# Rank rotation of gathered keys moved from the attention loop into a DRAM table built in the setup

## The reference, cut to what matters

```
_, idx = jax.lax.top_k(I, kk)                      # kk = 96, local ones are +inf
key_c = (c_kv @ W_uk)[bi, idx]
value = (c_kv @ W_uv)[bi, idx]
kr_sel = (x @ W_kr)[bi, idx]                       # 32 numbers per key
angles_k = jnp.arange(kk)[:, None] * theta[None, :] + delta     # rank, not position
key_r = _pope(kr_sel, angles_k[None, None, :, :])
```

## Time and profile before

| | |
|---|---|
| time, median of 3 runs | 1587.76 us (1586.1 to 1593.62) |
| span of the profiled execution | 1577.7 us |
| busy PE, DVE, ACT, POOL | 1150.9 (73%), 839.3 (53%), 752.6 (48%), 533.3 us (34%) |
| gathers on POOL | 496, 491.9 us busy |
| setup of this layer | about 498 to 617 us |
| first and last `row_max` | 665.5 and 1419.1 us |

### The profile page before, as it was taken

How to read it: one execution, slowest core, us unless ns; L and a number is a source line. 1 busy time by engine, 2 the same in 40 slices (tenths; PEclk the granted TensorE clock), 3 DMA queues, 4 the chain that set the end, 5 groups by cost and what they waited for, 6 DMA issues and landing times. The chain is left out here.

```text
span 1577.7 us, 20354 instructions
## 1 busy us (share of the span) xinstructions
PE 1150.9 (73%) x6768; PEld 804.0 (51%) x6768; DVE 839.3 (53%) x1759; ACT 752.6 (48%) x1801; POOL 533.3 (34%) x532
## 2 busy tenths in 40 slices
PE   6639958996999676367686776876777748287897
PEld 2138825672666222255564555655555536174554
DVE  2075555534553566466665665656556546034536
ACT  4722336771875544255444454445445434074425
POOL 2000000000000448366666666666666653600000
PEclk8559978995999566576656767667666555578999
DMA  5000000000003235112222122222222212200000
GB/s 181 0 1 0 0 0 0 1 0 0 1 1 87 76 90 139 46 32 56 54 54 56 32 56 54 57 55 47 41 57 55 54 25 41 57 5 27 1 1 27
DMA packets 74367, 61.82 MB, mean 39 GB/s; under 512 B 31570, under 2 KB 58900, under 8 KB 73764
## 3 DMA queue, kind: packets, MB, share of 16 engines
q1 hardware_dynamic: 58404, 36.28, 9.3%
q0 software_dynamic: 15872, 24.41, 6.7%
HBM read 52.51 MB, written 8.13 MB: 38 GB/s over the span
## 5 line engine op out<-in xcount | busy, mean ns | idle before, releaser
L542 POOL DMA_INDIRECT arena_lo<-key_table,idx_T x496 | 491.9, 992 | 304.0 <-issue 134.8
L576 PE MATMUL bank<-arena_lo 128*32 128x32 f32 (+6 forms) x1656 | 208.5, 276 | 116.1 <-ACT arena_hi L1280 66.6
L576 PEld LDWEIGHTS bank<-arena_lo 128*32 128x32 f32 (+5 forms) x1656 | 177.7, 166 | 168.4 <-issue 131.2
L555 POOL TENSOR_TENSOR arena_lo<-arena_lo 128x512 f32<-128x512 f32 x8 | 11.8, 1474 | 516.4 <-DVE arena_lo L1608 516.1
L856 PE MATMUL bank<-ident,arena_hi 128*96 128x128 f32 x512 | 113.4, 363 | 24.4 <-DVE arena_hi L1700 23.2
L1254 ACT ACTIVATE arena_hi<-bank 96x512 f32<-96x512 f32 x128 | 74.7, 583 | 113.6 <-remote 67.3
L1280 ACT ACTIVATE arena_hi<-bank 32x128 f32<-32x128 f32 x128 | 33.5, 262 | 194.0 <-remote 160.7
L1668 DVE SCALAR_TENSOR_TENSOR arena_lo<-arena_lo,iw 128x512 f32<-128x512 f32 (+4 forms) x114 | 76.1, 668 | 81.5 <-ACT arena_lo L1237 46.2
L1237 ACT ACTIVATE arena_lo<-bank 128x512 f32<-128x512 f32 (+4 forms) x152 | 76.5, 512 | 65.7 <-remote 30.9
L576 PE MATMUL bank<-index_k_hi,index_q 128*128 128x512 f32 (+5 forms) x160 | 94.0, 589 | 18.7 <-issue 17.0
L1710 DVE CUSTOM_DVE_ANT_0 arena_hi<-bank,score_mask 128x208 f32<-128x208 f32 x124 | 46.4, 374 | 106.9 <-issue 71.0
(11 more groups left out here) (257 smaller groups left out, 2484.3 us busy)
## 6 DMA issues: line engine op xcount, KB each, us to landing
arena_lo<-key_table,idx_T POOLq DMA_INDIRECT x496
arena_lo<-q_l SPq DMA_DIRECT2D x64, 64.0 KB
arena_lo<-q_lat SPq DMA_DIRECT2D x32, 128.0 KB
arena_lo<-q_g SPq DMA_DIRECT2D x64, 64.0 KB
h<-in_h SPq DMA_DIRECT2D x2, 1024.0 KB, 8.2
q_l<-arena_hi SPq DMA_DIRECT2D x8, 256.0 KB
q_g<-arena_hi SPq DMA_DIRECT2D x8, 256.0 KB
q_lat<-arena_hi SPq DMA_DIRECT2D x8, 256.0 KB
```

The lines of the kernel that those rows point to most:

```text
L542: pool.indirect_dma_start(out=G[b][:, q, :], out_offset=None, in_=key_table[0:index_width(i), :], in_offset=bass.IndirectOffsetOnAxis(ap=i ...
L576: return pe.matmul(out_, lhsT, rhs, start=start, stop=stop, **kw)
```

## The change

A table `rank_table` in DRAM (65536 rows of 64 numbers, 16.8 MB) holds, for each of the 2048 keys, 32 rows: the key turned by each rank from 64 to 95, and its latent beside it. Gathers read from it by index*32 + rank. What it adds in the setup for each chunk: on PE one product with a combining matrix, four small ones for latents, and eight products of 128 keys by 512 columns (`rank_turn`); eight copies of 128x512 from PSUM, four on ACT and four on DVE; eight latent copies on POOL; eight stores of 512 KB. The four transposes of raw keys are gone. POOL issues the gathers of tile 0 in chunk 1 and those of tile 1 in chunk 2, ahead of its part of chunk 3. What it changes in the loop: `rows_rotate` and a small DVE operation behind the row maximum are gone; two transposes of row pairs take the place of four; the scores of a group use two products with zero-padded query blocks (`QGz`) in place of four; one copy of turned probabilities replaces two; rows are of 64 numbers, not 96. Queries are double-buffered, attention lags its slot by 2 and not 7, and the picks end in slot 114. In front of the loop ACT waits for all stores and regroups the queries of tile 0. Semaphores of the linear attention are shared with an earlier layer.

```diff
+            def store_rank_rows(k, r):
+                b = 2 * (k % 2) + r
+                sp.wait_ge(t_halfs[r], k + 1)
+                sp.wait_ge(t_latb, 2 * k + r + 1)
+                sp.dma_start(rank_table[k * P * JG:(k + 1) * P * JG, :]
+                             .rearrange("(p r) w -> p r w", r=JG)[:, r * JG // 2:(r + 1) * JG // 2, :], tab[b])\
+                    .then_inc(t_store_t[b], 16)
...
+                sp.wait_ge(t_lats, c + 1)
+                sp.dma_start(lat_table[c * C:(c + 1) * C, :].rearrange("(b p) r -> p b r", p=P), lat_rows)\
+                    .then_inc(t_store_v, 16)
+                for j in range(4):
+                    for r in range(2):
+                        store_rank_rows(4 * c + j, r)
+                if c == 0:
+                    first_rows()
...
                     pool.indirect_dma_start(
-                        out=G[b][:, q, :], out_offset=None, in_=key_table[0:index_width(i), :],
+                        out=G[b][:, q, :], out_offset=None, in_=rank_table[0:JG * index_width(i), :],
...
+                pool.wait_ge(t_lats, c + 1)
+                for j in range(4):
+                    k = 4 * c + j
+                    for r in range(2):
+                        b = 2 * (k % 2) + r
+                        if k >= 2:
+                            pool.wait_ge(t_store_t[b], 16 * (k // 2))
+                        pool.tensor_copy(tab[b][:, :, DR:ROW], lat_rows[:, j:j + 1, :].to_broadcast([P, JG // 2, DC]))\
+                            .then_inc(t_latb, 1)
+                if c in (1, 2):
+                    table_stored(pool, c)
+                    gather(c - 1)
+            table_stored(pool, NT)
...
                     pe.wait_ge(t_iqs, 5 * c + 4)
-                    pe.wait_ge(t_rawd, c + 1)
+                    pe.wait_ge(t_kro, c + 1)
+                    mm(bank[7][0:ROW, :], key_comb, kro).then_inc(t_kl, 1)
+                    pe.wait_ge(t_iqs, 5 * c + 5)
+                    keys = raw[c % 2]
                     for j in range(4):
-                        last = pe.transpose(bank[7][:, j * ROW:(j + 1) * ROW], raw[c % 2][:, j * P:(j + 1) * P],
-                                            ident[0:ROW, 0:ROW])
-                    last.then_inc(t_rows, 1)
+                        last = mm(bank[2][:, j * DC:(j + 1) * DC], keys[:, j * P:(j + 1) * P], rank_turn[:, JG * DR:])
+                    last.then_inc(t_lat, 1)
+                    for j in range(4):
+                        for r in range(2):
+                            if j == 0:
+                                pe.wait_ge(t_qlats, 2 * c + r + 1)
+                            else:
+                                pe.wait_ge(t_halfs[r], 4 * c + j)
+                            mm(bank[3 + r], keys[:, j * P:(j + 1) * P], rank_turn[:, r * C:(r + 1) * C])\
+                                .then_inc(t_half[r], 1)
...
             def rows_turn(n):
-                pe.wait_ge(a_rot, n + 1)
+                i, g = n // NG, n % NG
+                if n < FIXED // GQ:
+                    pe.wait_ge(fixed_rows, 16 * QD)
+                else:
+                    gathers = i // 2 + (i % 2 == 1 or g >= FIXED // GQ)
+                    pe.wait_ge(gathered[i % 2][g], 16 * GQ // QD * gathers)
                 if n >= 2:
                     pe.wait_ge(a_gts, n - 1)
-                for j in range(4):
-                    last = pe.transpose(bank[2 + n % 2][0:ROW, j * P:(j + 1) * P], GR[n % 2][:, j, :], ident[:])
+                for p in range(2):
+                    pair = G[i % 2][:, 4 * g + 2 * p:4 * g + 2 * p + 2, :].rearrange("p j r -> p (j r)")
+                    last = pe.transpose(bank[2 + n % 2][:, p * P:(p + 1) * P], pair, ident[:])
                 last.then_inc(a_gt, 1)
...
             def scores(n):
                 i, g = n // NG, n % NG
                 pe.wait_ge(a_gts, n + 1)
-                pe.wait_ge(a_q, 4 * i + g // 2 + 1)
+                pe.wait_ge(a_q, 4 * i + 4)
                 if n >= 3:
                     pe.wait_ge(a_otc, n - 2)
                 s0 = max(i * P + g * GQ - LW, 0)
                 sb_, w = score_bank(n), NH * QD
-                mm(sb_[:, P:KEYS], QL[:, g, :], KL[:, s0:s0 + WIN])
-                for j in range(4):
-                    last = mm(sb_[j * w:(j + 1) * w, 0:P], QG[:, g, j * w:(j + 1) * w],
-                              GT[n % 2][:, j * P:(j + 1) * P], tile_position=(0, j * w))
+                mm(sb_[:, P:KEYS], QL[i % 2][:, g, :], KL[:, s0:s0 + WIN])
+                for p in range(2):
+                    last = mm(sb_[2 * w * p:2 * w * (p + 1), 0:P], QGz[i % 2][:, 2 * g + p, :],
+                              GT[n % 2][:, p * P:(p + 1) * P], tile_position=(0, 2 * w * p))
                 last.then_inc(a_s, 1)
...
-                fn(PTl[n % 2], score_bank(n)[0:WIN, P:2 * P], ACT.Copy)
-                fn(PTg[n % 2], score_bank(n)[:, 0:P], ACT.Copy).then_inc(a_pts, 1)
+                fn(PT[n % 2], score_bank(n)[:, 0:2 * P], ACT.Copy).then_inc(a_pts, 1)
...
+                act.wait_ge(t_halfs[1], NT)
                 for s in range(SLOTS):
                     n = s - ATTN_LAG
-                    if n == -4:
+                    if s == 0:
                         act.wait_ge(t_store_l, STORES_L * (NCH + 1))
                         act.wait_ge(t_store_q, STORES_Q * (NCH + 1))
                         act.wait_ge(t_store_g, STORES_Q * (NCH + 1))
-                        act.wait_ge(t_store_k, STORES_K * (NCH + 1))
+                        table_stored(act, NT)
+                        for part_ in range(4):
+                            queries_regroup(0, part_)
                     if 0 <= n + 1 < GROUPS:
...
-            def rows_rotate(n):
-                i, g = n // NG, n % NG
-                if n < FIXED // GQ:
-                    dve.wait_ge(fixed_rows, 16 * QD)
-                else:
-                    gathers = i // 2 + (i % 2 == 1 or g >= FIXED // GQ)
-                    dve.wait_ge(gathered[i % 2][g], 16 * GQ // QD * gathers)
-                if n >= 2:
-                    dve.wait_ge(a_gt, n - 1)
-                v.tensor_tensor(GR[n % 2], G[i % 2][:, 4 * g:4 * g + 4, :],
-                                rank_rope[:].unsqueeze(1).to_broadcast([P, 4, ROW]), ALU.mult).then_inc(a_rot, 1)
...
-        ATTN_LAG = NG - 1
-        PICK_SLOTS = NG * NT - 10
+        ATTN_LAG = 2
+        PICK_SLOTS = NG * (NT - 2) + ATTN_LAG
```

More of the change, by code:

```diff
@@ L52 @@
 NEG = -1e30
+FAR = 1e30
+HIGHEST = 3e38
 LOWEST = -3e38
@@ L89, in shape_tables @@
     for name, a in (("qg", q_g), ("ql", q_l)):
-        t["cos_" + name] = np.tile(np.cos(a), (NH, 1)).astype(f32)
-        t["sin_" + name] = np.tile(np.sin(a), (NH, 1)).astype(f32)
+        t["cos_" + name] = (-SCALE * np.tile(np.cos(a), (NH, 1))).astype(f32)
+        t["sin_" + name] = (-SCALE * np.tile(np.sin(a), (NH, 1))).astype(f32)
     c, s = np.cos(q_g), np.sin(q_g)
-    t["key_rope"] = np.concatenate([c, c, -s, s]).astype(f32)
-    a = (LW + np.arange(JG))[:, None] * theta[None, :]
-    row = np.concatenate([np.cos(a), np.cos(a), -np.sin(a), np.sin(a), np.ones((JG, DC))], axis=1)
-    t["rank_rope"] = np.tile(row, (P // JG, 1)).astype(f32)
+    t["key_rope"] = np.concatenate([c, c, -s, s, np.ones((DC, T))]).astype(f32)
+    eye, none = np.eye(half), np.zeros((half, half))
+    comb = np.zeros((RAW, ROW))
+    comb[0:2 * DR, 0:DR] = np.block([[eye, none], [none, eye], [eye, none], [none, eye]])
+    comb[2 * DR:RAW, DR:ROW] = np.eye(DC)
+    t["key_comb"] = comb.astype(f32)
+    turn = np.zeros((RAW, JG * DR + DC))
+    for r in range(JG):
+        c, s = np.diag(np.cos((LW + r) * theta)), np.diag(np.sin((LW + r) * theta))
+        turn[0:2 * DR, r * DR:(r + 1) * DR] = np.block([[c, none], [none, c], [-s, none], [none, s]])
+    turn[2 * DR:RAW, JG * DR:] = np.eye(DC)
+    t["rank_turn"] = turn.astype(f32)
     r = np.arange(P)
@@ L103, in shape_tables @@
     first = np.broadcast_to(x < LW, (P, WIN))
-    t["score_mask"] = np.where(np.concatenate([own, near], 1), 0, NEG).astype(f32)
-    t["score_mask_first"] = np.where(np.concatenate([own, first], 1), 0, NEG).astype(f32)
+    t["score_mask"] = np.where(np.concatenate([own, near], 1), 0, FAR).astype(f32)
+    t["score_mask_first"] = np.where(np.concatenate([own, first], 1), 0, FAR).astype(f32)
     p, s = np.arange(P)[:, None], np.arange(KTOP)[None, :]
@@ L256, in hybrid_kernel @@
         ROPE = at[0]
-        rope_tab = [part(4, C) for _ in range(NCH)]
-        cq, raw = [part(C, parts=DCQ) for _ in range(2)], [part(C, parts=ROW) for _ in range(2)]
+        rope_tab = part(4, C)
+        SCRATCH = at[0]
+        cq, raw = [part(C, parts=DCQ) for _ in range(2)], [part(C, parts=RAW) for _ in range(2)]
+        q_abs, mu = part(2, C), [part(2, C) for _ in range(2)]
+        assert at[0] == SCRATCH + 5120
+        tab = [part(JG // 2, ROW) for _ in range(4)]
+        G = [part(P // QD, ROW)]
+        lat_rows = part(4, DC)
         k_abs = part(C, parts=2 * DR)
```

(9 more changed lines are left out.)

329 lines of the change are left out of this document (191 added, 138 removed).

## The result

The changed kernel takes 1670.68 us (median of 4, 1657.23 to 1678.67) where the kernel before takes 1587.57: a ratio of 1.051, 95% interval 1.047 to 1.055. It is slower, as forecast, but by 83 us and not by 25. The profiled execution has a span of 1667.9 us beside 1577.7, 90.2 us more; it took 1669.73, so 1.8 us lie around a span. The 10.1 us that the prediction added were mostly the profiled execution of before being a quick one, so about 7 of the 90.2 us are not in the medians.

What follows compares the result with a forecast made beforehand. The prediction took gathers, the longest leg, plus POOL's pauses for PE's late signals to bound the loop. Span 1577.7 + 67 (setup) - 36 (loop) - 6 (its end) = 1602.7, with 10.1 1612.8 us; range 1562 to 1660.

Steps and rivals of the forecast that it cites:

- The 10.1 us that the prediction added: Whole kernel: time around the profiled span, 1587.76 us median against 1577.7 us span, added at the end.
- Forecast +67: Setup: first row maximum at 732 us against 665.49, so +67 us, bounds +45 and +89.
- 12.5 us more each: Setup: each chunk takes 12.5 us more, between 9.0 and 17.1 us of added PE work.
- PE's part of a slot gets about 20% shorter, DVE's as much: Loop slots: lighter PE and DVE work shortens POOL's pauses, taken as 0.32 us a slot.
- -36 for the loop: Loop: 112 slots beside gathers save 36 us through shorter and rarer POOL pauses; bounds 0 and -105.
- -6 for its end: After the last gather: some 14 slots lose 0.4 to 0.5 us each, -6 us.
- The upper bound of the gain, 105 us: Loop: 112 slots going from 6.04 to 5.1 us if POOL never pauses again, -105 us.
- Bursts at tiles 14 and 15: Loop: late indices again make the 32 gathers come in one 40 us burst, two bursts as before; 0 change.
- D: Rival: setup worse, signals held beside tile 1's gathers, POOL's cycle stays; +89 - 10 - 6 = +73, 1660.9 us; 20%.
- B: Rival: loop's coupling of PE and gathers loosens, slots at POOL's 5.1 us; 67 - 105 - 6 = -44, 1543.7; 16%.
- C: Rival: setup's additions partly hidden in PE's idle time, +45; 45 - 36 - 6 = +3, 1590.9 us, no change; 14%.
- The reading of the kernel before: Loop: PE's signals arrive late while gathers are under way, and POOL's pauses let them through; mechanism unknown.

Runs made afterwards that it cites:

- e3: Changed kernel with tile 1's gathers moved behind POOL's last piece of the setup; 1.031 of the kernel before.
- e13: Changed kernel with a table of 16 ranks per key, half the size, its products in turn in two banks; 1.040 of the kernel before.
- e1: Kernel before without DVE's rank product, an 8-column product left in its place; 1410.83 us, 0.989 of the kernel before.
- e14: Kernel before with two of four gathers of a group from tile 2 on; 1360.74 us, 0.852 of the kernel before.
- e15: Changed kernel with two of four gathers of a group from tile 2 on; 1440.48 us, 0.895 of the kernel before.
- e16: Kernel before with POOL waiting for every eighth gather to land in tiles 1, 14 and 15; 0.981 of the kernel before.
- e5: Kernel before, unchanged, run again on a chip of the quick kind; 1417.18 us.
- e6: Changed kernel, unchanged, run again on a chip of the quick kind; 1497.11 us, 1.057 of the kernel before.

## Why the prediction failed in size

**The setup was right, and a little small.** Forecast +67, measured +74.5, inside its bounds of 45 and 89. Tile 1's gathers were to begin at 648 and began at 657.3; they, POOL's piece and the chain behind were to end in four regroups by 722 and a first row maximum at 732. The regroups ended at 730.2 and the first row maximum came at 740.0. All the 8 us were lost ahead of the gathers. I had put the three chunks at 12.5 us more each; they took 14.1 (81.8 us from the first rotation to tile 1's indices, 124.1 after), and the first began 6 us late, at 532.2, which the sum had not. e3 and e13 divide it in part: 29 us by the place of tile 1's gathers, and by an estimate some 28 by the size of the table. The two were never changed together and ran on different kinds of chip, and what the rest of the 74.5 is stays open.

**The step that failed is "PE's part of a slot gets about 20% shorter, DVE's as much", and with it -36 for the loop and -6 for its end.** Measured: +9.2 together, for -42. PE's part did not get shorter at all. At the same slow clock it is 3.30 us for 3.23, and over the eleven tiles beside gathers PE was busy 419 us for 395. The sum costed it by halving merged rows: eight narrow products in 0.66 us became four in 0.3. But the eight took only 0.43 from start to start. The new scores cost about 0.2 us more and not 0.3 less, and the product of the last 64 tokens went from 0.48 to 0.64; together that is more than the 0.29 that the two fewer transposes saved. Besides, the granted clock in the loop fell from 0.67 to 0.59, and from 0.73 to 0.65 on the quick chips, a term that the sum did not have. What it costs by itself no run shows. DVE's part did get shorter, but e1 puts the product at 13 to 16 us for the whole kernel where nothing is held. So the stream of gathers ran at its old pace: 536.3 for 538.2 us over eleven tiles; on the quick chip 574 for 577, where nothing pauses and a lighter slot could not show at all. e14 and e15 agree: with half of the gathers the first 39 steps have a mean of 4.27 and 4.24 us. The upper bound of the gain, 105 us, was worked out from a slot of 6.04 us that no row gives; the rows have 6.13 in the loop and 5.93 over all groups.

**The end of the loop** was to win 6 us and lost 13.3 from the first gather of tile 13 on. The last 13 steps took 46 us for 37, because the clock stayed at 1.2 GHz with PE 98% busy, where before it rose to 2.4: in the kernel before a step takes 3.2 to 3.4 us at the slow clock and 2.3 at the fast one. That, and 6.5 us in the layers behind at 0.84 for 0.90, are sizes the sum had at nothing. e15 shows the same end, 46.3 us for 33.3 in e14. What keeps the clock down there isn't settled: no run changed it alone. Bursts at tiles 14 and 15 came as forecast. Of the other 4 us, 3.4 lie ahead of tile 14's first gather: POOL waited 19.3 us for its indices and not 14.4.

**The rivals.** D came nearest, 10 us under the result, but not by its own terms: its +89 for the setup was measured as +74.5, its -10 and -6 as +9.2 for the whole loop, and another +6.5 lie behind it. Its reason for the setup was another, too: PE and ACT ran on beside tile 1's gathers from 657 to 671 us, and then waited for stores (41.09 us in ACT's row) and not for held signals; its piece about the loop, that the cycle stays, was what happened. It had been given 20%; the range left out its far part, and the result lies 11 us beyond. B is refuted twice: on the first chip the cycle stayed, and on the quick ones, where POOL does go at 5.1 us, it went so before the change as well. C fell with the first row maximum at 740.

**The reading of the kernel before** holds as far as it went: signals of PE reach the others late while gathers run, on such a chip. PE's timeline at the long wait of ACT:

```profile
1345.73 0.74 PE L576 MATMUL bank<-arena_lo 80*32 80x128 f32 x10
1349.79 0.47 PE L876 MATMUL bank<-ident,arena_hi 128*128 128x128 f32 x1 [3.33 <-issue]
1350.06 0.42 PE L877 MATMUL bank<-ident,arena_hi 128*80 128x128 f32 x1
1376.49 3.78 PE L576 MATMUL bank<-arena_hi,arena_lo 32*128 32x128 f32 x16 [26.01 <-ACT arena_hi L1280]
```

The row of x10 is `values`, over by 1346.5. ACT's copy of their output, which waits for PE alone, began at 1376.17. That pauses are what lets the signals through was argued from rows before. e16 bears it out, as 9 added waits took 32 us off, and so does e14. What the reading lacked is that this is no trait of every chip.

## What to carry to other kernels

Find the one stream that never stops (here 480 gathers at 1.25 us) and ask of a change first when that stream starts, how many entries it has, and where it gets a gap: work removed from any other engine is worth little until that is answered (in e1, some 1% of the time for DVE's whole rank product). Cost an array operation by the distance between starts, not by the duration of a merged row: a merged row can hide that its instructions ran beside each other, and half of its duration is then no price for half of them. And what is put in front of a long setup's end is to be placed in each in-order queue, POOL's and SP's, one after the other.

## What the runs showed of the hardware that was not expected

The kernel before takes 1414 to 1424 us on three chips and 1588 to 1603 on three others. The gathers themselves are alike on both kinds, 0.94 us and 0.30. The granted clock doesn't account for it: it is 0.739 in the kernel before on the first chip and 0.767 in e5, but 0.728 in e6, where the waits don't occur either. What differs is that signals of PE arrive late while POOL issues gathers, 26.4 us late in a burst of 28, and come through when POOL pauses for some 2 us. With half of the gathers, two in a row for a group, the effect is small (22 us of ACT's waits in e14 for 232). What holds them isn't in these traces. Besides, PE stayed at 1.2 GHz over 46 us in which it was 98% busy, and a slot of 20 PE instructions took as long as one of 26 at the same clock (3.30 and 3.23 us).
